# A GNN and mixture-of-experts kernel: when and where four experts' stored outputs are loaded back

## The reference, cut to what matters

```python
# _L2_ffn_ref: a graph attention with 4 heads x 4 numbers gives the gates
h = (x_flat @ W_gat).reshape(M, HEADS, NUM_EXPERTS)
e = leaky_relu(a_src[src] + a_dst[dst]); ee = exp(e - e_max[dst])
agg = segment_sum(h[src] * (ee / denom[dst]), dst) + b_gat
scores = _layernorm(agg, ln_gamma, ln_beta).reshape(M, HEADS, 4).mean(1)
w = softmax(top_k(scores, 2))
for ei in range(4):
    hh = gelu(x @ W1[ei] + b1[ei])
    out = out + g[ei] * (hh @ W2[ei] + b2[ei])
# then
x = x + out
x = x + _L3_gnn_ref(_layernorm(x), L3_gnn_W, src, dst, 2500)
```

## Time and profile before

| | us |
|---|---|
| median of the runs shown (3 runs, 6104.18 to 6139.05) | 6113.26 |
| span of the profiled execution | 6109.5 |
| stage 3, four-head attention, about | 4118 to 4586 |
| stage 4, scores and loads | 4586.1 to 4615.5 |
| stage 5, norm of L3 | 4615.5 to 4682.6 |

### The profile page before, as it was taken

How to read it: one execution, slowest core, us unless ns; L and a number is a source line. 1 busy time by engine, 2 the same in 40 slices (tenths; PEclk the granted TensorE clock), 3 DMA queues, 4 the chain that set the end, 5 groups by cost and what they waited for, 6 DMA issues and landing times.

```text
span 6109.5 us, 70270 instructions
## 1 busy us (share of the span) xinstructions
PE 4932.3 (81%) x23497; PEld 2951.4 (48%) x23497; DVE 3794.6 (62%) x7229; ACT 1630.4 (27%) x2765; POOL 3155.8 (52%) x2151
## 2 busy tenths in 40 slices
PE   5766666656889898989668979777766999999999
PEld 3444444434445575557566656673223333222266
DVE  6797668876676602130234520699996998777744
ACT  2111111112112201220122222127772002666521
POOL 5678888888888888888877877002220000000000
PEclk8878777777999998999877879889998999999999
DMA  7776666665444595559798866884433011222200
GB/s 191 153 143 137 122 128 122 129 96 63 6 11 18 18 125 33 16 7 125 83 191 89 90 51 72 175 174 121 112 102 74 29 29 28 82 81 82 79 11 28
DMA packets 558594, 523.44 MB, mean 86 GB/s; under 512 B 263641, under 2 KB 489874, under 8 KB 557159
## 3 DMA queue, kind: packets, MB, share of 16 engines
q1 hardware_dynamic: 295560, 427.91, 31.5%
q0 software_dynamic: 261696, 90.13, 23.7%
q10 hardware_dynamic: 1028, 1.52, 0.1%
HBM read 365.58 MB, written 153.75 MB: 85 GB/s over the span
## 4 chain that ended last, share of the span: by engine, by line
PE 52%; DVE 18%; issue 9%; SPq 7%; DMA 7%; POOL 6%; ACT 1%; DVEq 0%; ACTq 0%; POOLq 0%; PEldq 0%
SPq L188 6%; PE PS L2390 6%; PE PS L1448 6%; PE PS L1057 6%; PE PS L2227 5%; PE PS L1029 5%; DVE WORK L2031 4%; DVE MXS L2268 4%; PE PS L1754 3%; PE PS L1040 3%; DVE XT L545 3%; POOL sums L822 3%; DVE ROWS L545 2%; DMA WORK<-x_table,WORK 2%; PE PS L1254 2%
## 5 line engine op out<-in xcount | busy, mean ns | idle before, releaser
L760 POOL DMA_INDIRECT pairs<-PAIR_CNT,PAIR_IDX x1364 | 2150.1, 1576 | 491.2 <-issue 453.4
L545 DVE SCALAR_TENSOR_TENSOR XT<-PS,ROWS 128x1024 f32<-128x1024 f32 (+1 forms) x704 | 694.0, 1050 | 160.1 <-PE PS L515 159.7
L822 POOL DMA_INDIRECT sums<-WORK,XT x340 | 531.2, 1562 | 169.3 <-issue 100.8
L2461 DVE SCALAR_TENSOR_TENSOR WORK<-WORK 125x1000 f32<-125x1000 f32 x400 | 462.3, 1197 | 151.1 <-ACT WORK L2429 150.4
L632 PE MATMUL PS<-WORK,IDENT 125*125 125x256 f32 x680 | 277.3, 497 | 272.7 <-DMA WORK<-x_table,WORK 272.4
L2227 PE MATMUL PS<-ROWS 32*125 32x500 f32 x3200 | 451.0, 633 | 28.9 <-DVE MXS L2268 19.3
L2268 DVE TENSOR_REDUCE MXS<-PS 125x4 f32<-125x2000 f32 x200 | 438.9, 2236 | 24.1 <-PE PS L2248 20.0
L2019 POOL TENSOR_TENSOR WORK<-WORK,ROWS 125x500 f32<-125x500 f32 x100 | 126.0, 1260 | 630.8 <-ACT WORK L1983 630.8
L2429 ACT ACTIVATE WORK<-PS 125x1000 f32<-125x1000 f32 x400 | 380.0, 1002 | 237.8 <-PE PS L2378 237.8
L675 ACT ACTIVATE WORK<-PS 125x256 f32<-125x256 f32 x340 | 131.0, 385 | 1155.0 <-PE PS L632 1155.0
L515 PE MATMUL PS<-ROWS 128*128 128x512 bf16 x768 | 265.6, 471 | 212.0 <-DVE XT L545 154.3
(11 more groups left out here) (338 smaller groups left out, 8134.3 us busy)
## 6 DMA issues: line engine op xcount, KB each, us to landing
WORK<-pairs SPq DMA_DIRECT2D x400, 218.8 KB
pairs<-ROWS SPq DMA_DIRECT2D x75, 976.6 KB, 7.4
WORK<-pairs SPq DMA_DIRECT2D x48, 1093.8 KB
WORK<-pairs SPq DMA_DIRECT2D x80, 546.9 KB
pairs<-PAIR_CNT,PAIR_IDX POOLq DMA_INDIRECT x1364
WORK<-pairs SPq DMA_DIRECT2D x40, 382.8 KB
XT<-pairs SPq DMA_DIRECT2D x12, 1093.8 KB
mask_t<-ROWS SPq DMA_DIRECT2D x40, 273.4 KB
```

The source lines that it names most:

```text
L545: dve.scalar_tensor_tensor(junk[:, slot:slot + width // SUPER, :].rearrange("p a n -> p (a n)"), PS[:, bank + (0 if both else h):bank + (2 ...
L760: pool.indirect_dma_start(table, bass.IndirectOffsetOnAxis(idx[:, n:n + 1], 0), cnt[:, n:n + 1], None, compute_op=ALU.add).then_inc(sem(do ...
L822: pool.indirect_dma_start(sums[c], bass.IndirectOffsetOnAxis(SROW[:, k:k + 1], 0), SUMMED[:, k % 8, :], None, compute_op=ALU.add).then_inc ...
L2461: dve.scalar_tensor_tensor(E3[q % 8], E3[q % 8], 1.0, A3[n % 4][0:P].unsqueeze(1).to_broadcast([P, 2, CH]), ALU.min, ALU.mult).then_inc(se ...
```

## The change

The four stored outputs get other places, and all of them are loaded during the attention (stage 3), a piece at every second unit from t = 3 on in chunks 1 to 4:

- chunk 1: `outs_e[0]` in five pieces into XT, as before, its last tile into PAIR1_CNT; then four pieces of 2 tiles into PAIR_CNT and PAIR_IDX, which are no longer needed.
- chunk 2: tiles 0 to 7 of experts 1 to 3, one tile of all three at a time, into columns 0 to 767 of ROWS, which chunks 0 and 1 have read.
- chunks 3 and 4: fourteen pieces of 2 tiles into columns 768 to 1279 (chunk 3) and 1000 to 1511 or 1280 to 1791 (chunk 4).

Before each piece SP waits for `l2j_prob` to reach the count at which all units of the earlier chunks have been multiplied. The load of the counts of unit n follows behind the piece. Stage 4 keeps one issue of SP, that of the weights. VectorE reads the outputs from the new places and waits for other totals.

```diff
--- before.py
+++ after.py
@@ -1184,14 +1184,25 @@
         E_LATE, M_LATE = 4, 4
         outs_e = dram("outs_e", [E_LATE, N, D])
         O_ST = [ROWS[0:P, 4 + b, 0:4 * D].rearrange("p (t d) -> p t d", d=D) for b in range(4)]
-        OUTS = [XT[:].rearrange("p b n -> p (b n)")[0:P, 0:19 * D].rearrange("p (t d) -> p t d", d=D),
-                flat(WORK, 0, T, D)[0:P]]
-        OUTS += [ROWS[0:P].rearrange("p a b -> p (a b)")[:, 2 * N + q * T * D:2 * N + (q + 1) * T * D]
-                 .rearrange("p (t d) -> p t d", d=D) for q in range(2)]
-        OUT_LAST = ROWS[0:P].rearrange("p a b -> p (a b)")[:, 2 * N + 2 * T * D:2 * N + 2 * T * D + D]
+        OUTS0 = XT[:].rearrange("p b n -> p (b n)")[0:P, 0:19 * D].rearrange("p (t d) -> p t d", d=D)
+        OUT_LAST = PAIR1_CNT[0:P, 0:D]
+        EARLY_TILES = 8
+
+
+
+        OUTS3 = [ROWS[0:P, t, 0:3 * D].rearrange("p (e d) -> p e d", d=D) for t in range(EARLY_TILES)]
+        OUTS2 = [ROWS[0:P, r, at:at + 2 * D] for at, rows in ((1000, range(2)), (768, range(2, 8)), (1280, range(2, 8)))
+                 for r in rows]
+        OUTS2 += [v[0:P, q * 2 * D:(q + 1) * 2 * D] for v in (PAIR_CNT, PAIR_IDX.bitcast(F32)) for q in range(2)]
+        OUTS2 = [v.rearrange("p (t d) -> p t d", d=D) for v in OUTS2]
+        FREE_FROM = [4, 4] + [3] * 6 + [4] * 6 + [1] * 4
 
         def out_tile(e, t):
-            return OUT_LAST if e == 0 and t == T - 1 else OUTS[e][:, t, :]
+            if e == 0:
+                return OUT_LAST if t == T - 1 else OUTS0[:, t, :]
+            if t < EARLY_TILES:
+                return OUTS3[t][:, e - 1, :]
+            return OUTS2[(t - EARLY_TILES) // 2 * 3 + e - 1][:, t % 2, :]
 
         def outs_rows(e):
             return outs_e[e].rearrange("(t p) d -> p t d", p=P)
@@ -1292,17 +1303,25 @@
                                       ).then_inc(sem("l2e_copied"), 1)
             stage_end(dve)
 
-        def outs_ahead(sp):
-            spread(sp, "outs_loaded_first", OUTS[0], outs_rows(0)[:, 0:T - 1, :])
+        def outs_ahead(sp, c, i):
+
+            if c == 1 and i < NC:
+                some = slice(4 * i, min(4 * i + 4, T - 1))
+                spread(sp, "outs_loaded_first", OUTS0[:, some], outs_rows(0)[:, some, :])
+                if i == NC - 1:
+                    spread(sp, "outs_loaded_first", OUT_LAST, outs_rows(0)[:, T - 1, :])
+            if c == 2 and i < EARLY_TILES:
+                spread(sp, f"outs_loaded{i // 4}", OUTS3[i], outs_e[1:4].rearrange("e (t p) d -> t p e d", p=P)[i])
+            later = [j for j in range(len(OUTS2)) if FREE_FROM[j] == c]
+            i -= NC if c == 1 else 0
+            if 0 <= i < len(later):
+                t, e = EARLY_TILES + later[i] // 3 * 2, 1 + later[i] % 3
+                spread(sp, f"outs_loaded{t // 4}", OUTS2[later[i]], outs_rows(e)[:, t:t + 2, :])
+
+        OUTS_LOADED = [LOADED * (4 if c < 2 else 6) for c in range(NC)]
 
         def outs_sp(sp, then):
-
-            spread(sp, "outs_loaded_first", OUT_LAST, outs_rows(0)[:, T - 1, :])
-            for c in range(NC):
-                for e in (1, 2, 3):
-                    spread(sp, f"outs_loaded{c}", OUTS[e][:, 4 * c:4 * c + 4, :], outs_rows(e)[:, 4 * c:4 * c + 4, :])
-                if c == 1:
-                    ahead(sp, then)
+            ahead(sp, then)
             stage_end(sp)
 
         ECOL = sb("ECOL", [128, 4, 16])
@@ -1908,9 +1927,10 @@
 
         def l2j_sp(sp):
             for n in range(3, NC * T):
-                if n == T:
-                    outs_ahead(sp)
                 sp.wait_ge(sem("l2j_counted"), n - 2)
+                if n > T and n % T >= 3 and n % 2:
+                    sp.wait_ge(sem("l2j_prob"), n // T * T)
+                    outs_ahead(sp, n // T, (n % T - 3) // 2)
                 l2j_load(sp, n)
             stage_end(sp)
 
@@ -2147,12 +2167,12 @@
                 dve.scalar_tensor_tensor(C20[1][:, some], MEAN[:, some], -1.0, RSTD[:, some], ALU.mult, ALU.mult
                                          ).then_inc(sem("l3g_shift"), 1)
 
-            dve.wait_ge(sem("outs_loaded_first"), 2 * LOADED)
+            dve.wait_ge(sem("outs_loaded_first"), (NC + 1) * LOADED)
             for c in range(NC):
                 gated(c, 0)
                 if c:
                     shift(c - 1)
-                dve.wait_ge(sem(f"outs_loaded{c}"), 3 * LOADED)
+                dve.wait_ge(sem(f"outs_loaded{c}"), OUTS_LOADED[c])
                 for e in (1, 2, 3):
                     gated(c, e)
                 stats(c)
```

## The result

The changed kernel takes 6102.82 us in the median of 20 runs, the kernel before 6117.74 in 20 runs beside it: a ratio of 0.9973, with a 95% interval of 0.9963 to 0.9983. By the ratio that is 16.5 us less (10.4 to 22.6), by the medians 14.9: clear of chance with so many runs and still within 0.5%. One of the 20 runs of the changed kernel took 9249.12 us, for a reason that nothing here shows; the ratio leaves it out, and the median without it is 6102.73.

The account below looks back on a forecast made before the run. The prediction took 15 us at the end of the scores stage as bound by stored-output volume holding SP, and VectorE as busy throughout the attention. Terms -15.16 + 0 + 0 + 0 gave 6113.3 - 15.2 = 6098.1 us, range 6085 to 6114.

Parts of the forecast that it names:

- The stall is SP's queue at the barrier; 15.16 us go.: End of the scores stage: without 32 issues, the norm stage starts at 4600.34 in place of 4615.50, gaining 15.16 us.
- bound by the volume of the stored outputs: End of the scores stage: full queues hold SP, 7.8 MB at 240 GB/s taking 33 us; 15 us are stall.
- The attention carries the pieces for 0.: Attention: 64 issues in 31 pieces cost 0, since VectorE stays busy and SP and the queues have room.
- the 7.9 of the sum: Attention: lateness of counts behind a piece, 1.6 + 2.1 + 2.1 + 2.1 = 7.9 us against 11.6 of room.
- 242 GB/s as what the queues can carry: Attention: queue rate seen during the 19-tile load, set against 168 GB/s needed in chunk 1, the densest part.
- Cutting it up gains nothing.: Attention, chunk 1: splitting the load of 19 tiles gains nothing, as multiplications behind it stayed 4.51 us apart.
- that load cost nothing: Attention before the change: the 19-tile load made TensorE wait 1.81 us but cost VectorE nothing.
- rival 2: Attention, behind 31 pieces: counts over 15.4 us late cost up to 31 us per us beyond; chance 0.04.
- A fixed cost for each transfer: Attention: the skill's 2.0 us per transfer, if serial, would need 23.5 us per two units, giving 6548; judged excluded.
- The norm stage, the clock's term 0 +- 3.2.: Norm stage: same operations, 67.2 us, cost 0; TensorE's clock restart could shift it 3.2 us either way.
- The median, 6098.1.: Whole kernel: 6113.3 - 15.2 = 6098.1 us, 0.25% less; chance 0.84 for the forecast case.

Follow-up runs that it names:

- e1: Kernel before without the 32 issues of outputs 1 to 3 in the scores stage and nothing in their place; 6089.88 us, ratio 0.9972 to before.
- e2: Changed kernel with the fourteen pieces of chunks 3 and 4 issued in the scores stage again; that stage took 14.3 us.
- e9: Changed kernel with the fourteen pieces of chunks 3 and 4, then four mask loads for L3's maxima, in the scores stage; that stage took 16.82 us.
- e3: Changed kernel with the pieces of chunks 2, 3 and 4 issued in the scores stage again; that stage took 22.62 us.
- e6: Changed kernel with three further transfers behind every attention piece, four times the added volume; attention's first to last score 452.8 us.
- e7: Changed kernel with its first five pieces made one again, at t = 3 of chunk 1; attention's first to last score 452.0 us.
- e5: Changed kernel with one further transfer behind every attention piece, twice the added volume; attention's first to last score 447.1 us.
- e8: Changed kernel itself, run again on one chip beside a version with masks loaded in the scores stage; 6125.12 us, ratio 0.998 to before.
- e4: Changed kernel with the first four mask loads for L3's maxima issued in the scores stage behind the weights; 6087.41 us, ratio 0.9963 to before.

## Why the prediction was right, point by point

- *The stall is SP's queue at the barrier; 15.16 us go.* Right: 29.41 to 14.27, 15.14 us. The barrier cost 0.27 (0.25 foreseen), and e1, which only takes the stall away, gives the same ratio.
- *The stall was "bound by the volume of the stored outputs", 240 GB/s.* Right for the kernel before: ten issues took 1.48 to 2.16 us there, and the queues moved 236 GB/s from 4592 to 4615. It does not carry over to smaller pieces. In e2 and e9 nothing held SP, and what set its time, 0.44 us for each issue, is a term that the prediction's account of the stage does not have. e9 also shows SP free with 2.3 MB still to move: a barrier behind loads costs until the last one is accepted, not until it has landed.
- *The attention carries the pieces for 0.* Right: A 447.1 against 447.2, no count of TensorE waited for a transfer. So the counts were less than 11.6 us late, but whether by the 7.9 of the sum was not read off; only its first term was. The steps of the lateness can be read off the changed kernel's timeline at t = 3 of chunk 1, TensorE's count, VectorE's multiplication of the last unit of chunk 0, SP's first piece:

```profile
4228.55 1.94 PE L1943 MATMUL PS<-WORK,IDENT 125*125 125x500 f32 x4
...
4229.80 2.23 DVE L2057 SCALAR_TENSOR_TENSOR WORK<-WORK,PS 125x2000 f32<-125x2000 f32 x1
...
4232.11 0.83 SPq L188 DMA_DIRECT2D XT<-outs_e  x2
...
4234.31 2.23 DVE L2057 SCALAR_TENSOR_TENSOR WORK<-WORK,PS 125x2000 f32<-125x2000 f32 x1
```

  The count ended at 4230.49, the piece went at 4232.11: 1.6 us, as worked out from the earlier trace rows. Four such waits, at the four chunk starts, are the 17.8 us of L1932 above, of which 1.6 each are new.
- *242 GB/s as what the queues can carry* was mis-sized: they carried 274 in e3 and, with DRAM to DRAM traffic among it, 305 in e6. The margin was wider than the sum had it.
- *"Cutting it up gains nothing."* This step failed, though the forecast did not hang on it. It was read from a load that stood elsewhere, ahead of a unit whose counts did not wait for `l2j_prob`; at t = 3, with the last tile behind it, the lump costs VectorE 3.87 us. Even at its old place "that load cost nothing" was one profile's luck: in e1 it cost 0.5 us.
- *Late counts (rival 2)* did not happen. Its threshold of 15.4 us leaves out TensorE's clock. With the slow count (1.76 us more) the room is 13.6, and the 17.5 us of e7 give 3.9 over that, as measured; in e1, 12.9 us late, VectorE already lost 0.5 behind a slow count.
- *A fixed cost for each transfer*: there is none that adds up. e5 adds 64 issues for 0.0 us of A. The Trainium skill's "DMA: Bandwidth & Descriptors", section "Anatomy of one DMA", gives its 2.0 us for one transfer issued by GpSimd; it does not say that they add up over queued ones of SP, and here they do not.
- *The norm stage, the clock's term 0 +- 3.2.* 67.09 us before, 66.22 now. The groups of products in the changed kernel, first, second and third chunk, against the earlier trace rows:

```profile
4622.64 4.44 PE L2203 MATMUL PS<-WORK 128*125 128x256 f32 x16
...
4634.00 5.40 PE L2203 MATMUL PS<-WORK 128*125 128x256 f32 x16
...
4646.31 3.71 PE L2203 MATMUL PS<-WORK 128*125 128x256 f32 x16
```

  The first took 4.44 in place of 5.33, which is the 0.87 us, and with it nearly all that M gained beyond the scores stage (16.3 against 15.14). The fall of the clock behind it, the group of 5.40 us, costs the same in both kernels and only stands elsewhere. Since the first group varies from 4.21 to 5.76 us over the twelve profiles, 4.61 in e8 with the same kernel, one profile of each cannot tell the 0.87 from chance.
- *The median, 6098.1.* The difference came out as foreseen, 14.9 between the medians and 16.5 by the ratio against 15.2; the level was 4.7 higher because the three runs of before lay 4.5 under their later median of 20. That a change of 15 us could not be told from none was taken from the scatter of three single runs; with 20 runs of each it is clear.

## What to carry to other kernels

A stage that ends at a barrier of all engines is as long as its slowest engine, SP's issuing included: look at what SP still issues when the last engine is done, and at how long each issue takes. If they take their least time (here 0.3 to 0.5 us), their number sets the stage; if some take several times that, SP is held, and the amount does. Transfers moved under a busy stage cost nothing as long as what stands behind each piece still lands before its user, and that room is read from the trace (here 11.6 us for TensorE, 15.4 for VectorE, or 13.6 if TensorE's clock falls in the wait); one big piece uses up more of it than many small ones. Measure a change of 15 us from a fixed point just ahead of it and not by the span, when the stages upstream scatter by 49 us over executions and chips.

## What the runs showed of the hardware

- An issue of SP that is not held takes 0.30 to 0.47 us, be it of 13 rows or of 448 (changed kernel, e2, e4, e9). SP was held with 2.1 MB (before) and 1.8 MB (e3) of rows of 1 KB under way, in issues of up to 2.16 us, and was not held with 2.3 MB, mostly in rows of 5 KB (e9): it is something other than bytes that fills up.
- TensorE's granted clock falls once more in the norm stage, in eleven of the twelve profiles and at no fixed place: the slow group of 5.4 us is the fifth chunk's before, the second's in the changed kernel and the third's in e8_changed_beside, which is the same kernel. Its first three groups:

```profile
4653.30 4.61 PE L2203 MATMUL PS<-WORK 128*125 128x256 f32 x16
...
4664.83 3.71 PE L2203 MATMUL PS<-WORK 128*125 128x256 f32 x16
...
4675.45 5.40 PE L2203 MATMUL PS<-WORK 128*125 128x256 f32 x16
```

  Only e6_traffic_x4 has no such group; its first one is the longest of all:

```profile
4632.65 5.76 PE L2222 MATMUL PS<-WORK 128*125 128x256 f32 x16
```

  Its norm stage without that first group is 60.07 us, where it is 61.76 before and 61.78 in the changed kernel. So the dip costs 1.7 us, and it is not the change's.
